# A transformer block on one core: the FFN's rows of batches 2 to 4 turned by VectorE blocks and transfers in place of TensorE transposes

## The reference, cut to what matters

```
h = layernorm(x) * (1 + ca) + sa
x = x + ga * attention(h)
h = layernorm(x) * (1 + cb) + sb            # cb, sb: one value per batch and feature
shared  = relu(h @ W_up.T) @ W_down.T
logits  = h @ W_gate.T ; rw = softmax(top_2(logits))
x = x + gb * (shared + sum(rw) * (h @ W_expert))
```

## Time and profile before

| | |
|---|---|
| median of 3 runs | 401.78 us (401.06 to 402.11) |
| profiled execution, its own time | 400.71 us |
| span of the profiled execution | 398.9 us |
| TensorE busy / VectorE / ScalarE / GpSimd | 93% / 65% / 42% / 28% |
| mean granted TensorE clock | 0.966 of full speed |
| FFN of the four batches | from about 236 us to the end |

### The profile page before, as it was taken

The page is one execution under the profiler, slowest core; times in us unless marked ns, Lnnn a source line. Parts: engine busy times, 40 slices in busy tenths (PEclk is TensorE's granted clock), DMA queues, the critical chain, the costliest instruction groups (busy, mean ns, idle before and its releaser), DMA issues.

```text
span 398.9 us, 4661 instructions
## 1 busy us (share of the span) xinstructions
PE 371.0 (93%) x1664; PEld 288.7 (72%) x1664; DVE 260.5 (65%) x520; ACT 167.3 (42%) x293; POOL 110.4 (28%) x108
## 2 busy tenths in 40 slices
PE   4997979295999899999999999998999999999996
PEld 0146858284787687888888878886788878887885
DVE  0768899567797868988597665683751556084354
ACT  1237354765533781137602774217313711361120
POOL 0115063266283252932353240640001000100000
PEclk9987999688899999999999999999999999999999
DMA  7987961004001100000000001100200020011002
GB/s 226 403 328 246 359 268 55 0 0 151 9 2 45 35 0 2 22 6 0 2 0 28 0 0 54 53 28 0 79 28 0 27 81 0 0 55 53 2 0 105
DMA packets 10950, 27.42 MB, mean 69 GB/s; under 512 B 1184, under 2 KB 1568, under 8 KB 9776
## 3 DMA queue, kind: packets, MB, share of 16 engines
q1 hardware_dynamic: 10928, 27.13, 19.1%
HBM read 22.90 MB, written 4.23 MB: 68 GB/s over the span
## 4 chain that ended last, share of the span: by engine, by line
PE 73%; DVE 7%; issue 5%; DMA 5%; ACT 4%; POOL 3%; SPq 2%; POOLq 0%; DVEq 0%; ACTq 0%
PE ps L1035 21%; PE ps L1036 21%; PE ps L1037 21%; PE ps L1059 3%; PE ps L1042 3%; DMA gate_bc<-mod_rows 3%; DMA xs<-in_wmod 2%; DVE w_lo L615 1%; ACT sqj L444 1%; PE ps L1050 1%; PE ps L1162 1%; PE ps L1163 1%; POOL xs L349 1%; POOL hb L347 1%; DVE hb L659 1%
## 5 line engine op out<-in xcount | busy, mean ns | idle before, releaser
L1035 PE MATMUL ps<-w_hi,t_hi 128*128 128x512 f32 x192 | 76.0, 396 | 2.3 <-DVE prod L704 2.2
L1036 PE MATMUL ps<-w_lo,t_hi 128*128 128x512 f32 x192 | 75.2, 392 | 0.0
L1037 PE MATMUL ps<-w_hi,t_lo 128*128 128x512 f32 x192 | 75.2, 392 | 0.0
L1035 PE MATMUL ps<-w_hi,g_hi 128*128 128x512 f32 (+1 forms) x132 | 52.4, 397 | 4.2 <-DVE g_lo L745 4.2
L1035 PE MATMUL ps<-t_hi,w_hi 128*128 128x512 f32 x128 | 51.8, 405 | 0.0
L1036 PE MATMUL ps<-w_lo,g_hi 128*128 128x512 f32 (+1 forms) x132 | 51.5, 390 | 0.0
L1037 PE MATMUL ps<-w_hi,g_lo 128*128 128x512 f32 (+1 forms) x132 | 51.5, 390 | 0.0
L1036 PE MATMUL ps<-t_lo,w_hi 128*128 128x512 f32 x128 | 50.6, 395 | 0.0
L1037 PE MATMUL ps<-t_hi,w_lo 128*128 128x512 f32 x128 | 50.4, 394 | 0.0
L685 DVE TENSOR_TENSOR t_lo<-ps,t_hi 128x512 fp32r<-128x512 f32 x32 | 21.9, 687 | 37.2 <-ACT t_hi L495 37.1
L1035 PEld LDWEIGHTS ps<-w_hi,t_hi 128*128 128x128 f32 x192 | 36.5, 190 | 10.9 <-issue 3.4
(11 more groups left out here) (130 smaller groups left out, 616.6 us busy)
## 6 DMA issues: line engine op xcount, KB each, us to landing
xs<-in_X SPq DMA_DIRECT2D x4, 1024.0 KB, 7.8
stage<-in_w SPq DMA_DIRECT2D x4, 1024.0 KB, 6.0
out<-xs SPq DMA_DIRECT2D x15, 256.0 KB, 2.0
xs<-in_wmod SPq DMA_DIRECT2D x3, 1024.0 KB, 10.1
xs<-in_wmod SPq DMA_DIRECT2D x8, 256.0 KB, 6.5
stage<-in_w SPq DMA_DIRECT2D x8, 256.0 KB, 9.6
gate_bc<-mod_rows SPq DMA_DIRECT2D x8, 256.0 KB, 6.7
gate_bc<-in_wmod SPq DMA_DIRECT2D x1, 1024.0 KB, 12.7
```

The source lines that it names most:

```text
L1035: mm(dst, l_hi, r_hi, start=start, stop=False)
L1036: mm(dst, l_hi, r_lo, start=False, stop=False)
L1037: return mm(dst, l_lo, r_hi, start=False, stop=stop)
```

## The change

The transposes of the FFN's turns (g = 5, 6, 7) leave TensorE. In their place VectorE turns each row tile in 32 x 32 blocks (`turn`, one instruction of 128 x 512 for each tile, into the second half of `hb`); then sixteen transfers of SyncE, issued once all four tiles are turned, move the blocks between partitions, from `hb` back into `z`, which then holds features on partitions (`z_feat`). Each transfer goes from 32 partitions to 32 partitions, 4 pieces of 128 floats (512 B) on each, 64 KB in all. ScalarE's `z_evac` waits for all sixteen and then does what `t_evac` did, but reads `z_feat` instead of PSUM and writes its scaled result into PSUM.

To have the rows ready, the statistics and the normalisation move ahead. VectorE does the four `x2_rows` and `h_aggr` at the head of `ffn(b)` and `h_shift` ahead of the first `u_split`; two `turn`s follow the third `u_split` and two the fourth. ScalarE normalises two tiles after the first `u_evac` and two after the second. The `e_evac`s and `z_evac`s stand in the order e 0, e 1, z 0, z 1, e 2, z 2, z 3, e 3. SyncE issues a batch's sixteen transfers ahead of its four stores. VectorE's tail of `ffn(b)` (t_split and d_evac) and GpSimd's list are as before.

```diff
@@ -186,6 +186,7 @@
         eg_s = sem("eg_s")
         last_out = sem("last_out")
+        zq_s, zf_in = sem("zq_s"), sem("zf_in")
         out_dma = sem("out_dma")
@@ -203,6 +204,10 @@
         def h_row_of(g, t):
             return hb[:, g % 2, t, :]
+
+        QD = P // 4
+        z_blocks = hb[:, 1].rearrange("p t d -> p (t d)").rearrange("p (f t i) -> p f t i", f=4 * NC, t=NT)
+        z_feat = z[:].rearrange("p c s -> p (c s)").rearrange("p (c q t i) -> p c q t i", c=NC, q=4, t=NT)
         def kv_pair(b, t):
@@ -300,9 +305,15 @@
             load_gate_b(B - 1)
-            for i in range((B - 1) * NT):
-                sp.wait_ge(out_s, i + 1)
-                sp.dma_start(out_rows[i], xs[:, i * D:(i + 1) * D]).then_inc(out_dma, 16)
+            for b in range(B - 1):
+                sp.wait_ge(zq_s, b * NT + NT)
+                for q in range(4):
+                    for j in range(4):
+                        sp.dma_start(z_feat[j * QD:(j + 1) * QD, :, q].rearrange("p c t i -> p c (t i)"),
+                                     z_blocks[q * QD:(q + 1) * QD, j:4 * NC:4].rearrange("p c t i -> p c (t i)")).then_inc(zf_in, 16)
+                for i in range(b * NT, b * NT + NT):
+                    sp.wait_ge(out_s, i + 1)
+                    sp.dma_start(out_rows[i], xs[:, i * D:(i + 1) * D]).then_inc(out_dma, 16)
             for i, (t, part, _) in enumerate(LAST_PARTS):
                 sp.wait_ge(last_out, i + 1)
@@ -494,6 +505,29 @@
                 nc.scalar.activation(t_hi[:, g % 2, c, :], whole, ACT.Copy).then_inc(t_his, 1)
+            def z_evac(g, c):
+
+                n = g * NC + c
+                if c == 0:
+                    act.wait_ge(zf_in, (g - B) * 256)
+                act.wait_ge(t_los, n - 1)
+                j = (g - B) * NC + c
+                whole = ps[:, T_BANKS[c % 2], :]
+                nc.scalar.activation(whole.rearrange("p (t q i) -> p t q i", t=NT, q=4),
+                                     z_feat[:, c].rearrange("p q t i -> p t q i"), ACT.Identity,
+                                     bias=sb_col[:, j:j + 1], scale=cb_col[:, j:j + 1]).then_inc(t_full, 1)
+                act.wait_ge(t_full, n + 1)
+                nc.scalar.activation(t_hi[:, g % 2, c, :], whole, ACT.Copy).then_inc(t_his, 1)
+
+            def normalise_next(g, t0, n):
+                if t0 == 0:
+                    act.wait_ge(hnm_s, g * NT + NT)
+                    act.wait_ge(t_ps, (B + 1) * NC)
+                    act.wait_ge(t_full, g * NC)
+                for t in range(t0, t0 + n):
+                    nc.scalar.activation(z[:, t, :], xs[:, tok(g - B, t)], ACT.Identity, bias=hnm[:, t:t + 1],
+                                         scale=hrs[:, t:t + 1]).then_inc(z_s, 1)
+
             def q_evac(b, c):
                 n = b * NC + c
@@ -578,19 +612,21 @@
                 for c in range(NC):
                     u_evac(b, c)
+                    if not last and c < 2:
+                        normalise_next(b + B + 1, 2 * c, 2)
                     if c == 1:
                         act.wait_ge(top_s, b * 5 + 5)
                         nc.scalar.activation(tex[:], tdif[:], ACT.Exp).then_inc(ex_s, 1)
+                e_evac(b, 0)
+                e_evac(b, 1)
                 if not last:
-                    normalise(b + B + 1, 0, NT)
-                for c in range(NC):
-                    if not last:
-                        t_evac(b + B + 1, c)
-                    if c % 2 or last:
-                        e_evac(b, c // 2 if not last else c)
+                    z_evac(b + B + 1, 0)
+                    z_evac(b + B + 1, 1)
+                e_evac(b, 2)
                 if not last:
-                    e_evac(b, 2)
-                    e_evac(b, 3)
+                    z_evac(b + B + 1, 2)
+                    z_evac(b + B + 1, 3)
+                e_evac(b, 3)
             split_hi(4)
@@ -990,19 +1026,28 @@
                 v.tensor_tensor(xs[:, tok(b, t)], xs[:, tok(b, t)], y, ALU.add).then_inc(out_s, 1)
+            def turn(g, t):
+
+                dve.wait_ge(z_s, g * NT + t + 1)
+                v.transpose(z_blocks[:, :, t, :], z[:, t, :].rearrange("p (f r) -> p f r", r=QD)).then_inc(zq_s, 1)
+
             def ffn(b):
                 last = b == B - 1
+                if not last:
+                    for t in range(NT):
+                        x2_rows(b + B + 1, t)
+                    h_aggr(b + B + 1, 0, NT)
                 for c in range(NC):
+                    if c == 0 and not last:
+                        h_shift(b + B + 1, 0, NT)
                     u_split(b, c)
                     if c == 0:
                         routing(b)
-                    if not last:
-                        x2_rows(b + B + 1, c)
                     if c == 1:
                         routing_sum(b)
-                if not last:
-                    h_aggr(b + B + 1, 0, NT)
-                    h_shift(b + B + 1, 0, NT)
+                    if c >= 2 and not last:
+                        turn(b + B + 1, 2 * c - 4)
+                        turn(b + B + 1, 2 * c - 3)
                 dve.wait_ge(gb_in[b], 16)
                 for c in range(NC):
@@ -1186,10 +1231,6 @@
                 for t in range(2 if b == 0 else 0, NT):
                     expert_rows(b, t)
-                if not last:
-                    pe.wait_ge(lg_s, b * 2 + 1)
-                    transposes(b + B + 1, 0)
-                    transposes(b + B + 1, 1)
                 whole = [(t, slice(0, D), D_BANKS[t % 2]) for t in range(NT)]
                 for i, (t, part, bank) in enumerate(LAST_PARTS if last else whole):
@@ -1203,9 +1244,6 @@
                                      w_hi[:, WDOWN, k, part], w_lo[:, WDOWN, k, part], k == 0, k == NC - 1)
                     done.then_inc(d_ps, 1)
-                    if t == 0 and not last:
-                        transposes(b + B + 1, 2)
-                        transposes(b + B + 1, 3)
             for b in range(B):
```

## The result

The changed kernel takes 419.97 us, the median of 4 runs (417.87 to 422.45), against 401.94 for the kernel before: 1.0445 times as long, 95% interval 1.0376 to 1.0515. The forecast was 413.0, with a range of its own of 408 to 418 (chance 0.63) and 406 to 422 for 8 times in 10: the time lies outside the first and inside the second. As in the prediction, T is the end of U in a batch and s the start of `z_evac`.

The account below looks back on a forecast made before the run. TensorE's own list was taken to bound the FFN. The places' 7.72 + 4.0 - 0.25 - 0.25 gave 11.2 us more, a median of 413.0; own range 408 to 418, 8 times in 10 between 406 and 422.

Parts of the forecast that it names:

- What goes: Transposes and z wait leaving TensorE's list: 3.64 us in batch 1, 1.86 each in batches 2 and 3, 7.36 together.
- First place: U of batch 1: u_split waits behind h_shift for GpSimd's power, 5.12 us plus 2.6 of lower clock, 7.72 together.
- Second place: The rows' way through turns and transfers, every batch: 4.0 us more in batch 1, 0.25 less each in batches 2 and 3.
- the chain: From z_evac's start s to D's banks: first free for TensorE at s + 4.08, second at s + 8.8.
- its stand-in: One-input VectorE instructions of 128 x 512, 0.68 us long, taken as the length of a turn.
- the estimate of 1.24: Alternative turn length on VectorE, four times 311 ns: last turn some 1.5 us later, sum 417.5.
- eight in a row went out 0.47 apart: SyncE's issue pace taken for the sixteen transfers: last issue at T + 9.8, z_evac at T + 11.85.
- The fourth's own wait of 1.6: In batches 2 and 3, D's fourth tile waits 1.6 us for its bank, until T + 20.65.
- Third place: U of batches 2 and 3: low part ready about half a microsecond before U's third tile wants it; costed at nothing.
- the clock fell: Contradicts the rival that both long gaps in batch 1 leave the clock at 1.00: 8.0 us more, 409.8; chance 0.08.
- the transfers were not quick: Contradicts the rival that all sixteen land by T + 6.8 and no bank is late: 402.1, no change; chance 0.06.
- The rival of pieces of 512 B: Second place: 512 B pieces cost as much as 2 KB rows, s = T + 14.2, sum 18.3, 420.1 us; chance 0.20.

Follow-up runs that it names:

- the last version: Changed kernel with GpSimd's power ahead of W_down's low parts, earlier turns, d_evac 0 and 1 ahead, and transfers split between SyncE and ScalarE: 394.99 us (0.9849).
- the first two runs: Changed kernel with GpSimd's power of g = 5 ahead of W_down's low parts: 411.89 us; kernel before with only VectorE's statistics and h_shift moved ahead: 406.93 us.
- the run of long pieces: Changed kernel with each of the sixteen transfers as one piece of 2 KB a partition instead of four of 512 B: 417.55 us.

## Why the prediction was right, and where its sizes were off

- **What goes, 7.36 us:** held; in the last version the three stages are shorter by just that.
- **First place, forecast 7.72, measured 6.6:** the wait was 4.89 (5.12), by the cause named, shown from both sides by the first two runs. The clock fell as said and cost 1.6 us in the profiled execution for 2.6. One gap of the trace before was too little to price it by: the same gap cost from 1.6 to 3.0 in seven executions, so 2.6 lies within.
- **Second place:** the chain held to a tenth: TensorE has D's first bank 4.09 us after `z_evac`'s start (290.92 less 286.83; 4.08 forecast) and the second after 8.79 (335.29 less 326.50; 8.8 forecast). The turn took 0.686 us (0.68 by its stand-in; the estimate of 1.24 took four times the 311 ns that the Trainium skill, VectorE: DVE Perf Modes, section The three transpose paths, gives for 128 x 128 in bf16: for float32 tiles of 128 x 512 the measurement decides). The landing was 2.0 as taken. The one term that was mis-sized is "eight in a row went out 0.47 apart": the row was of loads from device memory, and these issues were 0.65 apart. That puts s at T + 14.45 to 14.6 for T + 11.85, and since each microsecond of s counts three times, batch 1 lost 6.5 for 4.0, batches 2 and 3 lost 2.5 each for a gain of 0.25. 3 x 2.6 = 7.8, less the 1.1 of the first place, is about the step from 11.2 to 18, and it is why the narrower range, 408 to 418, was missed.
- **A wait not forecast:** with s that late D's third tile waits in batches 2 and 3 too, 2.05 us each; forecast was only the fourth's. The fourth's own wait of 1.6 came in batch 2 (1.70); in batch 3 the clock's fall took its place.
- **Third place, cost nothing:** held, 13.34 us as before.
- **The rivals:** the clock fell, the transfers were not quick. The rival of pieces of 512 B came out at 420.1, nearly the time measured, but by luck: its reason is refuted by the run of long pieces, 0.59 us an issue against 0.60. The Trainium skill, DMA: Bandwidth & Descriptors, section Why small descriptors are slow (HBM only), says that transfers within the on-chip memory do not suffer from small pieces. This case agrees: with pieces of 512 B and of 2 KB a transfer landed in 2.0 us.
- **Open:** the runs of the changed kernel spread from 417.87 to 422.45 at granted clocks of 0.954 to 0.938; the profile is of the fastest, and what the others did in the gaps was not seen. That the same gap costs from 1.6 to 3.0 us, and that a gap of 2 us may or may not bring the lower clock, could make part of this spread, but no trace of those runs shows it.

## What to carry to other kernels

Work taken off the bounding engine pays only if its replacement arrives on time, so write the new chain from its trigger to each consumer's deadline, and look for what stands behind the new wait in the same engine's list: here it was always something else (a `u_split`, a `d_evac`) that TensorE missed first. A moved step also moves its waits: check each producer's list for what stands ahead of the thing waited for. Count the issues of many small transfers as work of the issuing engine, take their price from transfers of the same kind, and split them over two engines if the sum is on the path.

## What the runs showed of the hardware

At 64 KB an issue on SyncE takes 0.59 to 0.60 us for a transfer from the on-chip memory into itself, with pieces of 512 B or 2 KB and on 32 or 128 partitions, and 0.42 from device memory into it; on ScalarE, beside SyncE, the former took 0.63. Transfers within the on-chip memory landed in 2.0 us. A turn of 128 x 512 float32 in 32 x 32 blocks on VectorE takes 0.69 us, as long as its passes in `d_evac` and `t_split` (0.68 to 0.69). A gap of TensorE of 4.84 to 4.89 us brought the lower clock each time and cost from 1.6 to 3.0 us of the work behind it; of two gaps in the changed kernel the one of 2.06 us brought it and the one of 2.05 did not. `h_shift` on 128 x 4 numbers, 0.16 us long alone, lasted 1.16 beside GpSimd's pass over 128 x 512.
